# An accumulating gather issued one tile behind its source rows in place of two, in a two-layer graph network kernel

## The reference

```python
h = relu(layernorm(x))
feat = concatenate([h[src], h[dst]], axis=1)          # 8192 x 2048
e_hh = relu(feat[:256] @ W_hh + b_hh)
e_oo = relu(feat[256:1536] @ W_oo + b_oo)
e_ho = relu(feat[1536:] @ W_ho + b_ho)
logit = concatenate([e_hh, e_oo, e_ho]) @ W_a + b_a
alpha = softmax of logit over the edges of one dst
z = segment_sum(alpha * h[src], dst)
x = x + relu(concatenate([h, z], axis=1) @ (W_hn for the first 128 nodes, W_on for the others) + bias)
h = relu(layernorm(x))
x = x + normalised_adjacency @ (h @ W.T + b)
```

## Time and profile before

| | us |
|---|---|
| median of 3 runs | 643.06 (639.37 to 648.28) |
| the profiled execution's own time | 643.92 |
| its span, first to last instruction | 641.8 |
| PE, DVE, ACT, POOL busy | 564.2, 458.1, 309.3, 176.1 |
| gathers' stretch, first gather issued to last landed | 76 to 423 |

### The profile page before, as it was taken

One profiled execution on the slowest core, in us unless ns is written; L12 is line 12 of the kernel. 1 busy time (PEld: TensorE's weight loads), 2 busy tenths in 40 slices (PEclk: granted clock), 3 DMA queues, 4 the chain that ended last, 5 costly groups with the idle time before them and its releaser, 6 DMA issues.

```text
span 641.8 us, 8249 instructions
## 1 busy us (share of the span) xinstructions
PE 564.2 (88%) x2372; PEld 416.1 (65%) x2377; DVE 458.1 (71%) x975; ACT 309.3 (48%) x491; POOL 176.1 (27%) x165
## 2 busy tenths in 40 slices
PE   0799999999879997998988996657797999989997
PEld 0688777777546775765666664423577777868885
DVE  6716147678795887999999696768685449888452
ACT  2613312113159997648474565659673346324210
POOL 2000110075453665465655535500002000000000
PEclk9899999999898999899999998868987899999999
DMA  8335364389999999999999999944233537602111
GB/s 325 117 120 190 106 226 139 130 225 380 331 295 335 286 327 345 291 332 358 348 339 310 327 326 306 306 103 136 81 118 133 214 108 267 214 0 66 65 74 59
DMA packets 55975, 140.52 MB, mean 219 GB/s; under 512 B 6275, under 2 KB 6403, under 8 KB 55939
## 3 DMA queue, kind: packets, MB, share of 16 engines
q0 software_dynamic: 20624, 74.98, 38.1%
q1 hardware_dynamic: 27072, 50.34, 23.0%
q10 hardware_dynamic: 8242, 14.75, 6.2%
HBM read 123.27 MB, written 16.78 MB: 218 GB/s over the span
## 4 chain that ended last, share of the span: by engine, by line
PE 46%; DVE 21%; DMA 18%; ACT 7%; issue 5%; POOL 2%; ACTq 1%; DVEq 0%; POOLq 0%
PE ps L668 29%; DMA gath<-tab_b,tabl_i 12%; PE ps L618 4%; DVE gath L946 4%; PE ps L798 4%; PE ps L851 3%; ACT onehot L494 3%; DVE ring_l L921 3%; DMA gath<-tab_a,tabl_i 3%; PE ps L829 3%; DVE gath L941 2%; PE ps L757 2%; DMA raw<-in_L_gnn_W_on_dram 1%; DVE onehot L963 1%; ACT ring_h L447 1%
## 5 line engine op out<-in xcount | busy, mean ns | idle before, releaser
L668 PE MATMUL ps<-ring_h,actT_h 128*128 128x512 f32 x520 | 229.5, 441 | 9.8 <-DVE ring_l L921 5.3
L668 PE MATMUL ps<-ring_h,actT_l 128*128 128x512 f32 x520 | 208.6, 401 | 0.0
L668 PE MATMUL ps<-ring_l,actT_h 128*128 128x512 f32 x520 | 208.2, 400 | 0.0
L494 ACT ACTIVATE onehot<-onehot,lgs 128x512 bf16<-128x512 bf16 x192 | 124.6, 712 | 67.3 <-DVE onehot L963 65.0
L447 ACT CAST ring_h<-raw 128x512 fp32r<-128x512 f32 x176 | 103.8, 614 | 94.6 <-PE ps L668 72.7
L921 DVE TENSOR_TENSOR ring_l<-raw,ring_h 128x512 fp32r<-128x512 f32 x176 | 117.7, 685 | 36.3 <-ACT ring_h L447 36.2
L668 PEld LDWEIGHTS ps<-ring_h,actT_h 128*128 128x128 f32 x520 | 101.3, 195 | 45.5 <-DVE ring_l L921 6.9
L668 PEld LDWEIGHTS ps<-ring_h,actT_l 128*128 128x128 f32 x520 | 100.8, 194 | 23.0
L618 PE MATMUL ps<-onehot 128*128 128x512 bf16 x290 | 84.1, 399 | 35.1 <-ACT onehot L494 30.5
L668 PEld LDWEIGHTS ps<-ring_l,actT_h 128*128 128x128 f32 x520 | 101.4, 195 | 20.4
L301 POOL DMA_INDIRECT gath<-tab_a,tabl_i x64 | 71.8, 1122 | 149.5 <-DVE gath L946 69.4
(11 more groups left out here) (172 smaller groups left out, 508.8 us busy)
## 6 DMA issues: line engine op xcount, KB each, us to landing
raw<-in_L_gnn_W_ho_dram SPq DMA_DIRECT2D x32, 256.0 KB, 4.0
raw<-in_L_gnn_W_oo_dram SPq DMA_DIRECT2D x32, 256.0 KB, 4.9
raw<-in_L_gnn_W_hh_dram SPq DMA_DIRECT2D x32, 256.0 KB, 7.1
raw<-in_L_gnn_W_on_dram SPq DMA_DIRECT2D x32, 256.0 KB, 4.8
raw<-in_L_gnn_W_hn_dram SPq DMA_DIRECT2D x32, 256.0 KB, 4.1
tab_a<-stage ACTq DMA_DIRECT2D x24, 256.0 KB, 7.6
tab_b<-stage ACTq DMA_DIRECT2D x24, 256.0 KB, 7.0
raw<-in_L_gnn_W_dram SPq DMA_DIRECT2D x16, 256.0 KB, 3.2
```

The costliest lines, as they stand in the source:

```text
L494: ins = nc.scalar.mul(onehot[:, s, 1 + i, :], onehot[:, s, 1, :], lgs[:, i, q:q + 1])
L668: mm = nc.tensor.matmul(ps[:, first + m, :], w, v, start=(k == 0 and i == 0), stop=(k == KT - 1 and i == 2))
```

## The change

The distance between the source gather of the loop and the accumulating gather that it issues is one tile in place of two:

```diff
-            LAG = 2
+            LAG = 1
             FIRST = 5
```

## The result

| | before | after |
|---|---|---|
| median, us | 642.63 (639.37 to 648.28, 4 runs) | 663.04 (660.4 to 665.1, 4 runs) |
| profiled execution, its span | 643.92, 641.8 | 663.95, 661.8 |
| last accumulating gather landed | 422.6 | 441.7 |
| from there to the end of the span | 219.1 | 220.0 |

The changed kernel takes **1.034 times** as long (95% interval 1.0296 to 1.0383), 20.4 us more; forecast were 662 us. The profiled spans differ by 20.0 us, and 19.1 of these lie ahead of the landing of the last gathered tile.

A forecast was written before the change was run, and what follows sets the result against it. Busy DMA engines (share 1.00) were taken as the bound. A later start, 26 loops of 9.89 us and the last gathers put the last landing 18.1 us later: 643.9 + 18.1 = 662 us, range 642 to 677.

The forecast's parts named there:

- What bounds it: Stretch of gathered tiles, 125 to 425 us: DMA engines have no idle time (share 1.00), DVE nearly none; DVE holds POOL.
- The loop: POOL's gathers, one even tile's source gather to the next: landing, step, accumulating issue, gap; 9.89 us a pair against 9.25.
- S(8): POOL's plain gather of tile 8's source rows (L301): to be issued at 155.29 us, 5.5 us later than before.
- A's issue: POOL's issue of an even tile's accumulating gather (L315), a term of the loop: 1.56 us.
- The start: First moved gathers on POOL: tile 6's accumulating gather stays at 153.35 us, tile 8's source gather comes 5.5 us later.
- The end: Last gathers, tiles 60 to 63: last landing at 440.7 us against 422.64, so the last tile comes 18.1 us later.
- Nothing behind absorbs it: After the last gather's landing, the chain of waits runs on unbroken, so the 18.1 us delay reaches the end.
- The waits: POOL's waits for source rows rise from 9.5 to near 100 us, for slots fall from 69.4 to under 20.
- No difference: Rival: L between 7.1 and 7.5, the loop costs a few us, earlier accumulating gathers return some; 644 to 655 us; 0.24.
- L: In the loop, time to landing of a source gather right behind an accumulating gather, with POOL then waiting: taken as 7.77 us.
- Much slower: Rival: landings stay as at the start (10.53 us), loop 12.65 us, end 95 us later, 739 us; chance 0.05.
- Faster: Rival: DVE's waits for accumulating gathers shrink, the loop does not bind; 12 us less, 632 us; chance 0.10.

The follow-up runs named there:

- the kernel with every other pair: Kernel before, with the accumulating gather moved ahead of the next pair's source gather at every second pair only (14 of 28 swaps): 636.53 us, 0.994.
- the kernel with D in the loop: Changed kernel with the accumulating gather also issued ahead of the odd tile's destination gather: 701.45 us, 1.0917 times the kernel before.
- Without the sum: Accumulating gather made a plain one, even tiles' sum left out: 627.83 us on the kernel before (LAG = 2), 627.14 us with LAG = 1.

## Why the prediction was right, point by point

**What bounds it: right in the main.** In the kernel before POOL was held by DVE; after, it is held by its own loop, as foretold. That the DMA engines were at their limit was put too strongly: from 165 to 380 us they moved 325 GB/s before, and 333 in the kernel with every other pair. Nor do they fall far behind it after: the DMA share was to be 0.94 and is 0.97. What was wrong there is the base: 0.94 was worked out from the mean of 125 to 425 us, 1.00, for the stretch from 165 to 380 us. That had a share of its own in the kernel before:

```profile
165.00:380.00 215.00, 196.15 (x808) 135.87 (x807) 186.59 (x395) 141.37 (x217) 118.51 (x93) 0.95 1.02 325
```

1.02 x 9.25/9.74 = 0.97.

**The loop: right in its length, by two errors that cancel.** 9.89 us a pair were forecast; 9.88 came, over the 26 pairs from S(8) to S(60). But A's issue, taken as 1.56 us from single rows, is 1.70 in the mean of A(8) to A(58), 0.14 more; the mean of the same A in the kernel before, 1.68, was there to be read. The time to landing, taken as 7.77, is 7.61 in the mean of these 26 turns (7.50 from S(10) to S(50)), 0.16 less. Each error is about 4 us over 26 pairs, 0.6% of the time; that they cancel is luck.

Nor is the time to landing one number. 19 of the 26 landings take 5.8 to 8.2 us, the other 7 take 8.6 to 11.0, and the median is 7.10. In the chain that ended last:

```profile
185.88 6.67 DMA gath<-tab_a,tabl_i
...
195.22 9.74 DMA gath<-tab_a,tabl_i
```

Just ahead of the second, from 190.31 to 193.43 us, ACT issues the four stores of a table half. From S(8) to S(58) there are seven such groups of stores, and each of the seven long landings is that of an S issued between 2.4 us ahead of and 5.4 us behind the last store of a group. The long landing of S(6), 10.8 us at the start, stands beside a group as well (149.87 to 152.99 us). No run here moves the stores, so that they make the landings long is likely, not shown.

**The start: mis-sized.** A(6) was to stay at 153.35 and S(8) to come at 155.29; they came at 154.92 and 158.10. S(6) itself was 1.29 us later (143.86 for 142.57), and A(6) took 2.88 us to issue. S(8) thus comes 8.4 us later than in the kernel before; 26 turns of 9.88 for 9.24 add 16.6, and S(60) is 25.0 later. **The end:** S(60) at 414.89 for 412.4, A(60) at 421.26 for 420.5, A(62) at 430.59 for 430.3, A(63) at 432.53 for 432.2, the last landing at 441.7 for 440.7. Of what was lost over the forecast at the start, 2.8 us, all but 1.0 came back here, since S(60) and S(62) landed in 6.1 and 6.75 us. The sum was 18.1 us, and the trace shows 19.1; that it is so near is luck in part, as these errors have both signs.

**Nothing behind absorbs it: right**, 219.1 us before and 220.0 after.

**The waits:** POOL for its rows near 100 us in over 20, came 114.8 in 28; POOL for slots under 20, came 2.3; DVE for gath<-tab_b about 50, came 56.9. The length of one, about 4 us, was right (114.8/28 = 4.1); only their number was put low, since nearly every moved A waits.

**The rivals.** *No difference* was tied to L between 7.1 and 7.5, and L of 7.1 or less was named as a sign of being wrong. The median of L is 7.10, but the loop goes by its mean, 7.61, and 7.50 in the middle, on the edge of the condition; its time, 644 to 655, did not come. The condition did not say which L is meant, and it held A's issue at 1.56. It should have been put on the whole loop, 9.25 us against what comes. *Much slower* did not come, as the landing at the start, 10.8 us for S(6), is not that of the rest; the kernel with D in the loop shows what a loop near that length costs (11.34 us a pair, 701.45 us), though there it is not the landing that is long. *Faster* has a true core that I gave too little room: an earlier A shortens DVE's waits, and brings 4 to 5 us where the swaps don't follow each other. The change as made can't show it, since it moves all 28.

**The rule that was set aside.** The estimate from the Trainium skill ("DMA: Bandwidth & Descriptors", Anatomy of one DMA), 3.2 us to landing, would have let the loop bind nothing. The trace of the kernel after disagrees, as that of before did: the landings of S in its chain take 5.8 to 11.0 us. Another section of this page of the Trainium skill, Rules for kernel authors, bears on the finding: issue a DMA early, compute, and wait for its semaphore late, so that its fixed cost overlaps. This case agrees where the loop is longer than the pace, and gives a price: a wait one tile sooner in POOL's order cost 20.4 us. Without the sum the same wait cost nothing (627.14 us for 627.83).

## What to carry to other kernels

When a wait for a transfer's landing stands ahead of the next transfer of the same kind on one in-order queue, add up the loop (landing, step, issue, gap) and hold it against the pace that the kernel keeps without it: the difference is paid once a turn, and to it comes what the first turn is late. Put a rival's condition on the whole loop, not on one term of it, and take each term as the mean over the instructions in the loop, not from one row. If a loop is too long, break it every second turn: here that was 4 us faster than the kernel before, where the loop closed at every turn was 20 slower.

## What the runs showed of the hardware that was not expected

An accumulating gather is dearer than a plain one in two places. POOL issues it in 1732 ns in the mean (33 of them, kernel before) and in 1097 when the same gather is made plain. And the DMA engines take longer over its packets. The page's row of the gathers' queue (packets, MB, share of 16 engines over the span), in the kernel without the sum and LAG = 2:

```profile
q0 software_dynamic: 20624, 74.98, 33.1%
```

In the kernel before, the same packets and bytes take 38.1%. 0.381 x 641.8 - 0.331 x 625.0 = 37.7 us of 16 engines, 603 us of one, over 33 x 128 = 4224 packets of 4 KB: 0.14 us more for each, where the mean over all 20624 packets without the sum is 0.16 us. So one accumulating packet costs nearly two plain ones by this estimate. The packet records of the traces agree: of the gathers' 4 KB packets, 13206 take 150 to 175 ns in the kernel before and 4039 take 325 to 350; without the sum it is 16842 and 67. The window of 125 to 425 us shows the same:

```profile
125.00:425.00 300.00, 269.17 (x1128) 184.69 (x1126) 263.96 (x563) 190.03 (x295) 141.84 (x124) 0.97 0.89 321
```

The DMA share falls from 1.00 to 0.89 while the bytes per second rise from 314 to 321 GB/s: a good part of what filled the stretch was the accumulating, not the bytes.
